# A decoder layer on one core: TensorE takes each attention group's row sums before its value products

## What is computed

```
q = rope(x @ Wq);  k = rope(x @ Wk);  v = x @ Wv          # 4 query heads share a group's k and v
scores = 30 * tanh((q @ k.T + alibi) / 8 / 30)
probs  = softmax(where(causal, scores, -inf))
x = x + (probs @ v) @ Wo + bo
```

## Time and profile before

| | us |
|---|---|
| median of 3 runs | 1178.95 |
| lowest and highest | 1177.77, 1179.72 |
| the profiled execution: its time | 1184.07 |
| its span, first to last instruction | 1182.3 |

### The profile page before, as it was taken

The page is one execution under the profiler, slowest core; times in us unless marked ns, Lnnn a source line. Parts: engine busy times, 40 slices in busy tenths (PEclk is TensorE's granted clock), DMA queues, the critical chain, the costliest instruction groups (busy, mean ns, idle before and its releaser), DMA issues.

```text
span 1182.3 us, 26989 instructions
## 1 busy us (share of the span) xinstructions
PE 1137.9 (96%) x10882; PEld 811.2 (69%) x10882; DVE 885.7 (75%) x1287; ACT 553.1 (47%) x617; POOL 657.6 (56%) x536
## 2 busy tenths in 40 slices
PE   4888999999999999999999999999999999999998
PEld 4665566656667676566666577777886776786683
DVE  6878887988979979788787688889745745654654
ACT  6766673754746737557466400000244543542441
POOL 1454394774855847649468389999342422423331
PEclk9999999999999999999999999999999999999999
DMA  9564334563455445544456267772002022012000
GB/s 322 153 184 137 121 102 151 155 189 110 132 154 173 118 152 152 184 120 129 133 165 209 94 124 150 146 148 66 1 19 48 7 55 54 18 35 54 19 19 36
DMA packets 166184, 134.15 MB, mean 113 GB/s; under 512 B 69629, under 2 KB 127363, under 8 KB 166083
## 3 DMA queue, kind: packets, MB, share of 16 engines
q1 hardware_dynamic: 141128, 126.44, 36.6%
q10 hardware_dynamic: 24960, 6.29, 3.7%
HBM read 81.76 MB, written 35.21 MB: 99 GB/s over the span
## 4 chain that ended last, share of the span: by engine, by line
PE 79%; DVE 9%; DMA 5%; issue 3%; ACT 2%; POOL 1%; SPq 0%; ACTq 0%; DVEq 0%; POOLq 0%
PE bank L963 13%; PE bank L1041 9%; PE bank L1042 9%; PE bank L701 9%; PE bank L702 8%; PE bank L703 8%; PE bank L789 5%; PE bank L1060 4%; PE bank L1059 4%; DMA unit_halves<-halves 3%; PE bank L791 2%; PE bank L779 2%; PE bank L782 2%; DVE halves L1598 2%; ACT region_c L1174 1%
## 5 line engine op out<-in xcount | busy, mean ns | idle before, releaser
L1985 POOL TENSOR_TENSOR parts<-parts 128x512 f32<-128x512 f32 x80 | 127.0, 1588 | 123.0 <-DVE parts L1446 123.0
L701 PE MATMUL bank<-hT_halves,w_hi 128*128 128x256 f16 x640 | 176.1, 275 | 8.6 <-ACT v_s L1121 4.2
L702 PE MATMUL bank<-hT_halves,w_hi 128*128 128x256 f16 x640 | 175.6, 274 | 0.0
L703 PE MATMUL bank<-hT_halves,w_lo 128*128 128x256 f16 x640 | 175.5, 274 | 0.0
L963 PE MATMUL bank<-kv,toep 128*128 128x288 f32 (+2 forms) x660 | 159.2, 404 | 0.7 <-ACT qT L1211 0.5
L963 PEld LDWEIGHTS bank<-kv,toep 128*128 128x128 f32 x660 | 124.5, 191 | 34.3 <-ACT qT L1211 0.8
L1990 POOL TENSOR_SCALAR_AFFINE_SELECT region_c<-region_c 128x512 f32<-128x512 f32 x128 | 108.6, 872 | 67.1 <-ACT region_c L1177 66.5
L2134 POOL TENSOR_TENSOR sqsum<-sqsum,toep 128x512 f32<-128x512 f32 x56 | 78.0, 1393 | 95.4 <-ACT toep L1353 95.3
L2003 POOL TENSOR_TENSOR ctx_lo<-ctx,ctx_hi 128x512 f16<-128x512 f32 x64 | 91.9, 1436 | 68.5 <-ACT ctx_hi L1153 67.0
L1174 ACT ACTIVATE region_c<-bank,cap_scale 128x1536 f32<-128x1536 f32 x64 | 98.3, 1536 | 36.7 <-PE bank L782 36.7
L1041 PE MATMUL bank<-odd_halves,guT 128*128 128x256 f16 x512 | 112.2, 273 | 0.0
(11 more groups left out here) (192 smaller groups left out, 2624.3 us busy)
## 6 DMA issues: line engine op xcount, KB each, us to landing
unit_halves<-halves SPq DMA_DIRECT2D x80, 256.0 KB, 2.2
q_both<-unit_halves SPq DMA_DIRECT2D x64, 256.0 KB, 2.8
q_high<-unit_halves SPq DMA_DIRECT2D x64, 128.0 KB, 3.0
toep<-kernel_padded SPq DMA_DIRECT2D x32, 256.0 KB, 4.0
wffn<-w_gu SPq DMA_DIRECT2D x6, 1280.0 KB, 6.9
cpair<-ctx_pairs SPq DMA_DIRECT2D x32, 176.0 KB, 4.7
xin<-x SPq DMA_DIRECT2D x8, 512.0 KB, 9.2
region_o<-wq SPq DMA_DIRECT2D x4, 1024.0 KB, 11.5
```

What stands on the lines that cost most here:

```text
L701: pe.matmul(dst, lh, rh, start=first and k == 0, stop=False)
L702: pe.matmul(dst, lh, rl, start=False, stop=False)
L703: mm = pe.matmul(dst, ll, rh, start=False, stop=last and k == n - 1)
L1985: pool.tensor_tensor(slot[:, 0], slot[:, 0], slot[:, 1], ALU.add).then_inc(unit_summed, 1)
```

## The change

`values` is written so that the sums, in either form, stand ahead of the products; all the waits now stand ahead of both. The products are issued by an inner function.

```diff
-                for v in range(2):
-                    mm = weigh(bank[:, pv_bank(g), v * S:(v + 1) * S], g % 3, lambda t: value_half(t, g, v))
-                mm.then_inc(pv_filled, 1)
+                def products():
+                    for v in range(2):
+                        mm = weigh(bank[:, pv_bank(g), v * S:(v + 1) * S], g % 3, lambda t: value_half(t, g, v))
+                    mm.then_inc(pv_filled, 1)
+
                 if first or g not in ADDED:
                     if NG * b + g:
                         pe.wait_ge(rsum_turned, NG * b + g)
                     weigh(bank[:, SUM_BANK, 0:S], g % 3, lambda t: sum_ones[:]).then_inc(sums_filled, 1)
+                    products()
                     return
                 pe.wait_ge(keys_added, len(ADDED) * (b - 1) + ADDED.index(g) + 1)
                 pe.wait_ge(rsum_turned, NG * b + g)
...
                 mm.then_inc(sums_filled, 1)
+                products()
```

## The result

The changed kernel takes 1186.6 us (median of 4 runs, 1184.96 to 1186.97) against 1178.42 for the kernel before, timed beside it: a ratio of 1.0052, 95% interval 1.0035 to 1.0068. So it is slower by about half a per cent, 6 to 8 us. The profiled execution of after took 1186.97 us with a span of 1185.2. Before's took 1184.07, 5.1 above its median, so the two traces differ by 2.9 us only.

The account below looks back on a forecast made before the run. TensorE, busy nearly all the time, was taken as the bound. The terms 4.25 + 0.54 + 2.75 - 0.35 - 0.1 = 7.1 us on the median 1178.95 gave 1186.05, forecast 1186.0 us, range 1180.6 to 1189.6.

Parts of the forecast that it names:

- The moved instructions: TensorE, each group: swapping products (1.31 us) and sums (0.54 us) costs nothing by itself; only waits move, 1.31 us earlier.
- longer lists of waits: All 64 groups: a further 0.05 us each at one instruction would add 3.2 us; the forecast took none of it.
- The wait in batches 1 to 6: Group 0: TensorE waits for GpSimd's key addition, 0.54 us in batch 1 and 0.85 in each of five others.
- The wait and the clock in batch 7: Group 0: TensorE idles 2.5 us, is 1.3 us later, and half clock behind it costs 1.8 us more.
- How much of batch 7 reaches the end: Up to the x2 transposes: the chain gains about 0.35 us, so batch 7 costs 2.75 us, 1.0 without the clock.
- The part of that wait that was to move ahead of group 6: Batch 7: the x2 wait splits, part moving ahead of group 6, whose sums wait for group 5's turn; total about the same.
- The normalisation buys nothing at the boundaries: VectorE's multiplication comes 1.2 us earlier, yet gains 0 at five of six batch boundaries and 0.1 us at one.
- The fifth rotation: VectorE at the batch's end: it waits longer for TensorE's fifth unit, near 1.3 us in place of 0.67.
- Batch 0: Two small waits, 0.19 and 0.16 us, go (-0.35 us); group 7's sums wait 1.3 us, swallowed by a later 4.59 us wait.
- No stall was swallowed: Rival: the 0.85 us stalls are absorbed at each next batch boundary, giving 1180 to 1182 us; chance 0.13.
- no boundary moved: Rival: each batch boundary gives back up to 1.2 us, 7.2 in all, giving 1175 to 1179 us; chance 0.08.
- first rival: Group 0's addition meets VectorE's wide work, 1.64 us more per steady batch, 1195 us; 0.17 for all times above 1188.

Follow-up runs that it names:

- group 0 left out: Changed kernel with sums first in all groups but group 0 of each batch, which keeps its products first: 1179.01 us, ratio 0.9988.
- the other four kernels with the wait: Changed kernel again (1.0064), sums first only in group 0 (1.0062), products first with waits ahead (1.0065), changed kernel with batch 7's group 0 products first (1.0035).
- all waits ahead: Kernel before, products still first, but the waits for the addition and VectorE's turn put ahead of them: 1188.32 us, ratio 1.0065.
- group 0 alone: Kernel before with sums first only in group 0 of batches 1 to 7, other groups and batch 0 unchanged: 1187.7 us, ratio 1.0062.
- the statistics moved: VectorE's find_below subtraction put behind row statistics (batch 7: also x2's); in changed kernel 1179.57 us (0.9998), repeated 1181.09 (1.0000); in before 1180.3 (1.0002).

## Why the prediction was right

Forecast were 1186.0 us in 1180.6 to 1189.6, slower at 0.80. The time is 1186.6, for the reasons given in the main, with two of the terms off in opposite directions.

**The moved instructions cost nothing: right.** With group 0 left out, the ratio is 0.9988, and sums and products follow one another without a bracket (303.73, 303.95, 304.17 in batch 3). The 3.2 us of longer lists of waits in all groups didn't come: where the waits are satisfied they cost nothing visible.

**The wait in batches 1 to 6: right in place and cause, too small by a fifth.** The brackets are 0.62 us in batch 1 and 0.87 to 0.88 in the others, next to the 0.54 and 0.85 predicted. But TensorE loses 1.04 us each, as worked out above. By the stretches S16 grows by 5.1 us between the two profiles and by 5.6 to 6.6 in the other four kernels with the wait, where 0.54 + 4.25 = 4.8 was forecast. What was mis-sized is the resumption. I took 0.05 us after the addition's end. In batch 3 it is 303.73 - 303.47 = 0.26, in batch 7 621.54 - 621.28 = 0.26, and in the kernel with the products first and all waits ahead 305.74 - 305.48 = 0.26 too. With the wait in its old place, behind the products, it is 0.06 in before (616.81 after 616.75), and 0.06 too in batch 7 of the kernel that puts back that group alone (620.94 after 620.88), whose other batches have 0.25 to 0.28. So the extra 0.2 us goes with the new place of the wait and its longer list, and not with what is computed after it. In the listing of before `keys_added` is the last of two, in that of after the first of five, and four more at the 0.05 us that I had set for one would be the 0.2. That this is how they are worked off is an inference: in the source the same wait is the first of two and the fourth of five, and no run separates the place from the number of waits. I had weighed such a cost for every group and rejected it by rows in which all waits were satisfied. It appears only where one is open.

**The wait and the clock in batch 7: right.** Predicted were 2.5 us of idling, half clock behind it, and TensorE later by 1.3 + 1.8 = 3.1 us from both. Seen: 2.53 us, half clock in all four profiles in which group 0 waits 2.5 us there (two of the changed kernel, group 0 alone, waits ahead), and 2.8 to 3.1 us by S7, 3.4 by the times.

**How much of batch 7 reaches the end: wrong, and it was worth 2 us.** The wait ahead of the x2 transposes was to stay as long as before, with its half clock. It fell to 0.91 us at full clock:

```profile
659.88 1.38 PE L864 MATMUL bank<-ident_s,hbuf 128*128 128x128 f32 x8 [0.91 <-ACT qT L1215]
```

The failed step is that "the chain gains 631.04 - 630.66, about 0.3 to 0.4 us". I followed the chain through VectorE and ScalarE to the last unit, where it is a few tenths, and took the transfer through DRAM as a constant. It is 4.61 - 2.16 = 2.45 us shorter, and the earlier trace rows hold only its end. The load of x2 behind it also lands 7.8 us after its issue in place of 10.0, and VectorE then no longer waits for that load but for GpSimd's row statistics:

```profile
652.18 3.04 DVE L1654 TENSOR_SCALAR hbuf<-x2r,ln_mv,ln_rstd 128x512 f32<-128x512 f32 x3 [3.76 <-POOL ln_rstd L1978]
```

So the head of the chain is another one than in the earlier trace rows. In the kernel with only batch 7's group 0 put back, the transposes start 38.3 us after the scores ahead of that group, against 40.7 in before, so this point is reached 2.4 us earlier. 2.19 - 0.91 = 1.3 of it come out of the wait itself, which is 0.91 there too. How much of this is the store's and how much the new order's is not separated. With group 0 alone and with all waits ahead the store is late (4.55 and 4.44 us), VectorE waits for the load again, and S7 is 1.2 and 1.5 us longer than in after; but with all waits ahead, and with the statistics moved in the new order (3.78 and 4.18 us), the wait at the transposes is 0.90 to 0.91 us all the same. The part of that wait that was to move ahead of group 6 shows in neither profile of the changed kernel; the two with the statistics moved in the new order have 0.56 us of it.

**The normalisation buys nothing at the boundaries: right, by a step earlier than I named.** The fifth rotation was to idle near 1.3 us in place of 0.67. In VectorE's timeline of after, at the end of batch 3, it is still 0.67:

```profile
356.33 0.69 DVE L1447 TENSOR_TENSOR parts<-bank,cos_s 128x512 f32<-128x512 f32 x1 [2.67 <-PE bank L703]
...
361.54 0.69 DVE L1447 TENSOR_TENSOR parts<-bank,cos_s 128x512 f32<-128x512 f32 x1 [0.19 <-PE bank L703]
...
364.16 0.69 DVE L1447 TENSOR_TENSOR parts<-bank,cos_s 128x512 f32<-128x512 f32 x1 [0.67 <-PE bank L703]
```

Before has 1.21, 0.19 and 0.67 at the same three rotations. VectorE's lead is used up at the first of these, where it waits for TensorE 1.46 us longer, and from there on everything hangs on TensorE. The boundary waits kept their size, as said. In group 4 of batch 3 the multiplication starts directly behind the products, 0.23 us of waiting for L791, as said; but VectorE's wait for the sums (1.03 us, predicted to be shorter than the 0.98 of the earlier trace rows) didn't shrink, because VectorE itself comes to it earlier.

**Batch 0: right on group 7, half right on the small waits.** Group 7's sums wait for the turn and the later wait swallows it:

```profile
95.18 0.64 PE L789 MATMUL bank<-region_c,sum_ones 128*32 128x256 f32 x8 [1.30 <-DVE region_c L1459]
...
103.28 0.49 PE L898 MATMUL bank<-wffn 128*128 128x128 f32 x2 [3.22 <-DVE wffn L1492]
```

1.3 us appear and 4.59 - 3.22 = 1.4 go. Of the two small waits that were to go, the 0.19 us did. The other, for `q_high` through DRAM, is 0.16 in before but 1.44 in after, and 1.29 with group 0 alone, where batch 0 is ordered as in before. So it varies by more than a microsecond without the change, and the 0.16 us are not shown to be gained.

**The rivals.** No stall was swallowed and no boundary moved. Of the first rival, the collision with VectorE's wide work, half is true, and I had read it off the wrong instruction. I looked at the addition, found it undisturbed in the steady batches (1.28 us), and concluded that VectorE was out of the way there. It was the select ahead of the addition that was held, 3.52 us for two in place of 1.74. So the collision is not an extra on top of the 4.25 us, it is their cause. The profile of before showed it, had I compared the selects of this group with those of another.

**The sum.** Forecast were 7.1 us. Worked out anew it is 5.95 for batches 1 to 6 (0.75 + 5 x 1.04), 2.8 to 3.1 for batch 7's group 0, less 2.4 at the x2 transposes and 0.3 in batch 0 (1.3 - 1.4, and the 0.19 of the earlier trace rows): 6.1 to 6.4, against 6.1 and 7.5 measured. The total was met partly because two errors of 1 to 2 us cancelled, and that is luck. The sum also leaves out the half clock behind the x2 transposes, which before's one profile has and after's two don't; how often before has it isn't known.

**Why the profiles differ by only 2.9 us.** By the stretches it is 474.07 - 468.95 = 5.1, less 48.16 - 46.86 = 1.3 in batch 7, less 0.6 ahead of batch 1 and 0.3 behind. Batch 7 of before is long in this profile: with the statistics moved, the same order on TensorE takes 45.23, which lacks the 1.0 us for the addition, and of the remaining 1.9 us 1.7 lie behind the start of the transposes (7.46 us from there to the end of S7 against 5.77), where the half clock is. That may be part of the 5.1 us by which this execution lies above before's median.

## What to carry to other kernels

When instructions change places on the engine that bounds the kernel, cost their waits: for each one, how long before the new place is it satisfied, and who holds up the one who satisfies it. If a wait turns out to be short of time by a microsecond, look one instruction further up on the producer for something that takes twice its usual time. And a chain that passes through a transfer must be read with that transfer's own landing times in it; here they were 2.16 us in one order and 4.61 in the other.

## What the hardware did that I had not expected

**The clock after a wait is not decided by the wait alone.** Before idles 2.19 us ahead of the x2 transposes and runs at 0.52 of the clock behind it. The same kernel with the statistics moved idles 2.18 us at the same place, and its transposes run at full clock, 1.37 us for eight (TensorE's timeline, and its windows):

```profile
655.28 1.37 PE L860 MATMUL bank<-ident_s,hbuf 128*128 128x128 f32 x8 [2.18 <-ACT qT L1211]
...
656.00:660.00 4.00, 3.98 (x36) 1.00 0.64 213
```

And the changed kernel with the statistics moved, in its second profile, dropped to the lower level after much shorter waits, in batch 3:

```profile
298.34 0.67 PE L779 MATMUL bank<-q_both,k_high 128*32 128x320 f16 x12 [1.15 <-ACT region_c L1178]
...
300.25 0.39 PE L701 MATMUL bank<-hT_halves,w_hi 128*128 128x256 f16 x1 [0.75 <-ACT v_s L1125]
...
300.00:303.00 3.00, 2.75 (x14) 0.53 0.78 229
```

A single profile shows only one outcome of this. The 2.5 us in batch 7 were followed by half clock in all four profiles that had them.

**Resuming took longer where the wait stands ahead of the whole group:** 0.26 us from the end of GpSimd's addition to TensorE's next start with five waits in the list, 0.06 behind the products with two.

**The late sixteenth of a store,** 2.16 or 4.6 us from the store's issue to the reload for the same 256 KB, above.
